# One Block instead of two, FFN weights turned by VectorE: an attention and FFN layer on one core

## The chip, the cores and the metric

The kernel runs on 1 core of one Trainium2 chip. The metric is the device time of one execution in microseconds. The engines of the core work side by side: PE (TensorE, matmul), ACT (ScalarE), DVE (VectorE), POOL (GpSimd) and SP (SyncE, which here only issues DMA transfers and waits for semaphores). Each engine runs its instructions strictly in order; a wait holds everything behind it on that engine.

## The reference, cut to what matters

```python
# x: (4, 512, 1024), ctx: (4, 64, 1024); 16 heads of 96 in 4 key/value groups
h = concat([ctx, layernorm(x)], axis=1)
q, k, v = layernorm(x) @ Wq.T, h @ Wk.T, h @ Wv.T
x = x + softmax(q @ k.T / sqrt(96)) @ v @ Wo.T
# FFN, INTER = 2752; w_gate, w_up: (2752, 1024), w_down: (1024, 2752)
def fake_quant(t, axis):
    s = maximum(max(abs(t), axis) / 127, 1e-8)
    return clip(round(t / s), -128, 127) * s
def qlinear(x, w):            # both sides scaled by row and rounded to integers
    return fake_quant(x, -1) @ fake_quant(w, 1).T
y = layernorm(x)
x = x + qlinear(silu(qlinear(y, w_gate)) * qlinear(y, w_up), w_down)
```

## The kernel before, in words

Everything is one launch with two phases, each a Block of its own with its own tensors in SBUF and PSUM; between the Blocks all engines meet.

**Attention** goes over 4 batches (one sequence of 512 tokens and 64 context rows each), and in a batch over 16 heads. Products of attention are done in three f16 matmuls (high and low halves: `three`, L819 to L821). A head has four tiles of 128 queries: scores (`score_tile`, L908 and L909) into one of two banks, VectorE's row maximum (L1117), ScalarE's exp (L1004), VectorE's reciprocal (L1122), GpSimd's scaling (L792), ScalarE's high half (L1015), GpSimd's low half (L797, L798), and a DMA transpose issued by SyncE (`turn_p`, L698), which the product with the values (`pv_tile`, L923 to L926) waits for. The projections of queries, keys, values and output of this and the next batch are spread between these (`side_work`).

**FFN weights are prepared beside attention.** There are 52 units: for each quarter of the intermediate columns 11 units of gate and up rows (`GU`; 10 of 128 rows and one of 96) with 1024 columns, and two of w_down rows with 2752 columns, which are worked in two halves of 1408 and 1344. A unit is loaded by SyncE (`stage`, L612), VectorE takes the row maxima (`tile_scale`, L1140) and from them the scale, ScalarE multiplies by its inverse and adds 1.5 x 2^23 (`lift`, L977), VectorE subtracts that constant and writes integers as bf16 (`round_off`, L1158), SyncE transposes them by DMA in blocks of 128 columns (`turn`, L653) and stores them in DRAM (`keep`, L664). There are 60 such pieces, 44 of 1024 columns and 16 halves. In the first batch four units are done, in the others 16 each, spread over the share of the batch that `WEIGHTS_FOR` names.

**What sets the order.** A planner at the head of the file gives each step a time on a modelled clock (`pe_times`, `stage_events`, `token_events`, `engine_events`) and sorts the steps by it, engine by engine (ACT_ORDER, DVE_ORDER, POOL_ORDER, SP_ORDER). The order of each engine's instructions is fixed by that; the times themselves are not kept.

**FFN** goes over 16 tiles of 128 tokens. The loops run so that the gates of tile t+2 come before the down product of tile t+1 on TensorE:

```python
gates(0, True)
gates(1)
down(0, True)
with pe.Fori(0, TILES - 2) as t:
    gates(t + 2)
    down(t + 1)
```

`gates` (L1388) has four quarters of three groups, each group 8 matmuls into one of four banks; the groups are 512, 512 and 384 columns wide (the last unit of a quarter has 96 rows, 32 columns of the third group are not read). `down` (L1401) has two halves of 22 matmuls. VectorE reads the groups with the scales (L1500, L1504, L1510, L1511), multiplies after ScalarE's Silu (L1429, L1520), takes maxima (L1525), rounds h (`h_part`, L1558, L1562), and does norm and rounding of a later tile between quarters (`x_stats`, `x_norm`, `x_quant`). SyncE loads tiles and transposes x and h by DMA (L1319, L1326). Ahead of the first gates stand, after the Block's start: 52 small transposes on TensorE and 17 copies on ScalarE that spread the weights' scales over all partitions (L1410, L1442), tile 0's norm, rounding and transpose, and the loads of the weights of quarters 1 to 3 (L1329) and of w_down (L1343). Quarter 0 is loaded in attention's last batch (`first_gates`).

Of the kernel before, what the change touches and what calls it, by code (L numbers as in the profile page):

```python
# [5 lines left out]
ALU = mybir.AluOpType  # L6
# [6 lines left out]
P = 128  # L13
B = 4
# [14 lines left out]
P_UP = 2.0 ** 9  # L29
SCALE = float(HD) ** -0.5  # L30
# [33 lines left out]
WEIGHTS_FOR = (1.0, 1.0, 1.0, 0.85)  # L64
# [3 lines left out]
PRO = VALUES + [("Q", 0, 0), ("Q", 0, 1)] + KEYS[:2] + [("Q", 0, 2)] + KEYS[2:4]  # L68
LATE_KEYS = [(*u, 0) for u in KEYS[4:]]
# [161 lines left out]

def stores_before(k, parity):
    return (k - parity + 1) // 2


LAND = 6.0
TOKEN_LEAD, TOKEN_STEP = 20.0, 10.0


def stage_events():  # L240

    act, dve, sp = [], [], []
    done, split, lifted, turned, kept = {0: 0.0, 1: 0.0, 2: 0.0, 3: 0.0}, 0.0, 0.0, [0.0], [0.0, 0.0]
    for n, (t, i) in enumerate(STAGE):
# [52 lines left out]
def engine_events():  # L297
# [3 lines left out]
    for b in range(B):  # L301
        for o in batch_order(b):
# [71 lines left out]

class Kept:


    def __init__(self, nc, ctx):
        def sb(name, shape, dt):
            return ctx.enter_context(nc.sbuf_tensor(name, shape, dt))  # L380

        self.ident = sb("ident", [P, P], F32)
        self.minus_half = sb("minus_half", [P, TT], F32)
        self.s_w = sb("s_w", [P, B * NUNIT], F32)
        self.w_first = sb("w_first", [P, 4 * QC * D], BF16)
        self.w_first_in = ctx.enter_context(nc.semaphore("w_first_in"))
        self.x2_out = ctx.enter_context(nc.semaphore("x2_out"))


def attention_phase(nc, x, ctxT, wqT, wkT, wvT, woT, w_gu, w_dn, x2, wq_c, wo_c, gu_q, dn_q, kept):  # L390
    with ExitStack() as ctx:
        def sb(name, shape, dt):
            return ctx.enter_context(nc.sbuf_tensor(name, shape, dt))

        def sem(name):
            return ctx.enter_context(nc.semaphore(name))

        def psum(name, shape, dt):
            return ctx.enter_context(nc.psum_tensor(name, shape, dt))

        ident, minus_half = kept.ident, kept.minus_half
        s_w, w_first, w_first_in, x2_out = kept.s_w, kept.w_first, kept.w_first_in, kept.x2_out
        x_acc = sb("x_acc", [P, TT, D], F32)
        xc = sb("xc", [P, 2, D], F32)
        xh = sb("xh", [P, 2, 2 * D], F16)
        stats = sb("stats", [P, 2, 6], F32)
        xnT = sb("xnT", [P, 2 * KD, S], F16)
        xnT_hi, xnT_lo = xnT[:, 0:KD, :], xnT[:, KD:2 * KD, :]
        w_in = sb("w_in", [P, 2, I], F32)
        wq2 = sb("wq2", [P, 2, 2, D], F16)  # L410
        wo2 = sb("wo2", [P, 2, 2, HALF], F16)

        wk_hi, wk_lo, wv_hi, wv_lo = [w_first[:, i * 3072:(i + 1) * 3072].bitcast(F16) for i in range(4)]
        q2 = sb("q2", [P, 2, 2, G, T], F16)
        k2 = sb("k2", [P, 2, KV, S], F16)
        v_hi = sb("v_hi", [P, ST, KV, HD], F16)
        v_lo = sb("v_lo", [P, ST, KV, HD], F16)
        p_f = sb("p_f", [P, NF, S], F32)
        p_nat = sb("p_nat", [P, NN, 2 * S], F16)
        pT = sb("pT", [P, 2, PB, T], F16)  # L420
        early = pT[:].rearrange("p j m t -> p (j m t)").bitcast(F32)
        early_wk, early_wq = early[:, 0:3072], early[:, 3072:3072 + D]
        ctx_in = xc[:, 0, 0:KD * C].rearrange("p (k c) -> p k c", k=KD)
        o2 = sb("o2", [P, 2, 2, QC, T], F16)
        o3 = sb("o3", [P, 2, T], F16)
        w_int = sb("w_int", [P, CUT], BF16)
        w_t = sb("w_t", [P, 2 * D], BF16)
        small = sb("small", [P, 48], F32)
        mean_var = small[:, 0:8].rearrange("p (t c) -> p t c", t=TT)
        var_eps, rstd = small[:, 8:12], small[:, 12:16]  # L430
        sums, inv_sum, neg_max = [small[:, a:a + 8].rearrange("p (j t) -> p j t", j=2) for a in (16, 24, 32)]
        w_amax, w_inv = small[:, 40:42], small[:, 42:43]

        ps_g = [psum(f"ps_g{i}", [P, 512], F32) for i in range(NG)]
        ps_s = [psum(f"ps_s{i}", [P, 1024], F32) for i in range(2)]
        ps_o = psum("ps_o", [P, 512], F32)

        consts = sem("consts")
        dconsts = sem("dconsts")
        x_in = [sem(f"x_in{t}") for t in range(TT)]  # L440
        acc_in = sem("acc_in")
        ctx_in_s = sem("ctx_in_s")
        w_in_s = [sem(f"w_in_s{i}") for i in range(2)]
        e_in = [sem(f"e_in{i}") for i in range(2)]
        e_up = sem("e_up")
        e_out = sem("e_out")
        h_up = sem("h_up")
        h_out = sem("h_out")
        w_up = sem("w_up")
        w_out = sem("w_out")  # L450
        w_small = sem("w_small")
        w_turned = sem("w_turned")
        w_stored = [sem(f"w_stored{i}") for i in range(2)]
        wq_kept = [sem(f"wq_kept{i}") for i in range(2)]
        wo_kept = [sem(f"wo_kept{i}") for i in range(2)]
        wq_in = [sem(f"wq_in{i}") for i in range(2)]
        wo_in = [sem(f"wo_in{i}") for i in range(2)]
        ln_st = sem("ln_st")
        ln_pow = sem("ln_pow")
        ln_y = sem("ln_y")  # L460
        x_hi_s = sem("x_hi_s")
        x_lo_s = sem("x_lo_s")
        xn_turned = [sem(f"xn_turned{t}") for t in range(TT)]
        g_done = sem("g_done")
        s_done = sem("s_done")
        mx_done = sem("mx_done")
        p_done = sem("p_done")
        p_high = sem("p_high")
        p_scaled = sem("p_scaled")
        p_low = sem("p_low")  # L470
        p_turned = [sem(f"p_turned{t}") for t in range(TT)]
        pv_done = sem("pv_done")
        ev_hi = sem("ev_hi")
        ev_lo = sem("ev_lo")
        q_moved = sem("q_moved")
        k_moved = sem("k_moved")
        ctx_hi = sem("ctx_hi")
        ctx_lo = sem("ctx_lo")
        v_up = sem("v_up")
        v_done = sem("v_done")  # L480
        inv_done = sem("inv_done")
        o_hi_s = sem("o_hi_s")
        o_lo_s = sem("o_lo_s")
        o_moved = sem("o_moved")
        acc_done = sem("acc_done")

        block = ctx.enter_context(nc.Block())

        def bank(use):
            return ps_g[AT[use] % NG]  # L490

        def filled(eng, use):

            eng.wait_ge(g_done, AT[use] + 1)

        def evacuated(eng, use):

            kind = use[1][0]
            if kind == "WO":
                eng.wait_ge(acc_done, ADDED[use] + 1)  # L500
            elif kind == "V":
                eng.wait_ge(v_done, VALUE[use] + 1)
            else:
                eng.wait_ge(ev_lo, SPLIT[use] + 1)

        def tile_no(b, t):

            return t if b is None else (b + 1) * TT + t

        def token_tile(b, t):  # L510

            return x_acc[:, t, :] if b is None else xc[:, t % 2, :]

        def halves(b, t):

            if b is None and t >= 2:
# [1139 lines left out]
```

## Time and profile before

| | us |
|---|---|
| median of 3 runs | 1663.08 |
| range of the runs | 1661.41 to 1667.41 |
| the profiled execution: its own time | 1660.82 |
| the profiled execution: its span | 1659.0 |
| attention's last output product added at | 1147.41 |
| a tile of the FFN's loop | 28.93 |

Busy times are those of each engine in the span or in a stretch; they overlap. A granted clock of 1.00 is TensorE's 2.4 GHz, and 0.5 is 1.2 GHz; a stretch's figure is a mean. The chain of waits is followed back from the last instruction, at each step to what released it; "SPq" in it is SyncE's queue, and "issue" is time in which the engine waited for nothing that the profile shows.

### The profile page before, as it was taken

To read this page: it belongs to the slowest core of one execution; us is meant where nothing else is said; L and a number is where in the kernel's file an instruction comes from. 1 tells how busy PE (TensorE), PEld (TensorE's weight loads), DVE (VectorE), ACT (ScalarE), POOL (GpSimd) and SP (SyncE) were. 2 spreads that over 40 slices of the span, in tenths; PEclk is the share of its full clock that TensorE was granted. 3 is DMA by queue.
4 is the path that set the end of the run, shared out by engine and by line. 5 is a ranking of instruction groups with operands and counts; after the bars stand their busy time and mean duration, and the time that the engine had idled before them with its cause. 6 is when DMAs were issued, how large, how long until landed. Compare 5 with 4: busy or idle time off the path is not lost.

```text
span 1659.0 us, 23906 instructions
## 1 busy us (share of the span) xinstructions
PE 1543.9 (93%) x8084; PEld 765.7 (46%) x8084; DVE 1031.0 (62%) x1952; ACT 644.0 (39%) x1180; POOL 637.7 (38%) x827
## 2 busy tenths in 40 slices
PE   6989989999988999999899899988599999999997
PEld 3544434654433465444355444444244444444443
DVE  5245564345574535566544557563589898998984
ACT  3366655146554315655523565562111111111110
POOL 3277786047766405767621576660000000000000
PEclk9999999999998999999999999999799999999999
DMA  7299999489999959999986999997923324233331
GB/s 247 69 247 230 232 251 238 145 222 229 247 234 224 243 170 220 234 224 257 235 208 188 285 241 255 207 232 213 364 62 81 104 65 102 80 82 103 81 92 56
DMA packets 529803, 310.92 MB, mean 187 GB/s; under 512 B 473904, under 2 KB 480816, under 8 KB 528560
## 3 DMA queue, kind: packets, MB, share of 16 engines
q1 hardware_dynamic: 529712, 309.76, 76.6%
q8 instruction: 50, 0.82, 0.2%
q14 instruction: 41, 0.34, 0.1%
HBM read 139.20 MB, written 46.66 MB: 112 GB/s over the span
## 4 chain that ended last, share of the span: by engine, by line
PE 62%; SPq 11%; DMA 9%; POOL 8%; ACT 4%; DVE 4%; issue 3%; ACTq 0%; DVEq 0%
PE ps_gu L1388 18%; PE ps_d L1401 10%; PE ps_g L819 8%; PE ps_g L821 8%; PE ps_g L820 8%; SPq L698 5%; PE ps_s L908 4%; POOL p_nat L797 3%; POOL p_f L792 3%; DMA pT<-p_nat 3%; PE ps_o L923 2%; PE ps_o L924 2%; PE ps_o L926 2%; SPq L680 2%; ACT p_nat L1015 1%
## 5 line engine op out<-in xcount | busy, mean ns | idle before, releaser
L797 POOL TENSOR_TENSOR p_nat<-p_f,p_nat 128x512 f16<-128x512 f32 x256 | 300.5, 1174 | 170.4 <-ACT p_nat L1015 169.4
L792 POOL TENSOR_SCALAR p_f<-p_f,small 128x576 f32<-128x576 f32 x256 | 205.3, 804 | 302.4 <-DVE small L1122 302.2
L1015 ACT ACTIVATE p_nat<-p_f 128x576 f16<-128x576 f32 x256 | 174.3, 681 | 243.6 <-POOL p_f L792 232.6
L908 PE MATMUL ps_s<-k,q 96*128 96x512 f16 x768 | 224.6, 385 | 40.5 <-ACT p_f L1004 40.4
L1117 DVE TENSOR_REDUCE small<-ps_s 128x1 f32<-128x576 f32 x256 | 191.8, 749 | 96.7 <-PE ps_s L909 95.8
L1004 ACT ACTIVATE p_f<-ps_s,small 128x576 f32<-128x576 f32 x256 | 186.8, 730 | 117.6 <-DVE small L1117 116.8
L1388 PE MATMUL ps_gu<-w_gu_sb,xT 128*128 128x512 bf16 (+1 forms) x1152 | 231.0, 361 | 1.0 <-DMA w_gu_sb<-gu_q 1.0
L1429 ACT ACTIVATE g_sb<-g_sb,sx 128x512 f32<-128x512 f32 (+1 forms) x128 | 74.5, 582 | 393.0 <-DVE g_sb L1500 336.1
L1367 POOL TENSOR_TENSOR rstd<-var_eps,minus_half 128x1 f32<-128x1 f32 x16 | 8.8, 548 | 458.5 <-DVE var_eps L1470 458.5
L1401 PE MATMUL ps_d<-w_dn_sb,hT 128*128 128x512 bf16 x704 | 162.5, 385 | 5.3 <-DMA hT<-h_int 5.3
L1388 PEld LDWEIGHTS ps_gu<-w_gu_sb,xT 128*128 128x128 bf16 x1152 | 112.7, 98 | 116.7 <-DMA w_gu_sb<-gu_q 1.4
L1122 DVE RECIPROCAL small<-small 128x1 f32<-128x1 f32 x256 | 40.6, 161 | 180.4 <-ACT p_f L1004 179.0
L819 PE MATMUL ps_g<-xnT,wq 128*128 128x512 f16 x384 | 147.6, 384 | 4.1 <-DVE wq L1070 2.2
L909 PE MATMUL ps_s<-k,q 96*128 96x64 f16 x768 | 148.5, 193 | 0.0
L819 PE MATMUL ps_g<-wo,o 128*128 128x512 f16 x384 | 147.8, 385 | 0.0
L923 PE MATMUL ps_o<-pT,v_lo 128*96 128x512 f16 x320 | 127.9, 400 | 21.1 <-DMA pT<-p_nat 19.5
L820 PE MATMUL ps_g<-wo,o 128*128 128x512 f16 x384 | 147.5, 384 | 0.0
L821 PE MATMUL ps_g<-wo,o 128*128 128x512 f16 x384 | 147.3, 384 | 0.0
L821 PE MATMUL ps_g<-xnT,wq 128*128 128x512 f16 x384 | 147.2, 383 | 0.0
L820 PE MATMUL ps_g<-xnT,wq 128*128 128x512 f16 x384 | 147.0, 383 | 0.0
L908 PEld LDWEIGHTS ps_s<-k,q 96*128 96x128 f16 x768 | 75.2, 98 | 140.4 <-issue 33.0
L1171 DVE SCALAR_TENSOR_TENSOR x_acc<-ps_g,x_acc 128x512 f32<-128x512 f32 x128 | 87.9, 687 | 62.6 <-PE ps_g L821 62.1
(113 smaller groups left out, 2467.7 us busy)
## 6 DMA issues: line engine op xcount, KB each, us to landing
w_in<-w_gu SPq DMA_DIRECT2D x40, 512.0 KB, 4.6
wq<-wq_c SPq DMA_DIRECT2D x36, 512.0 KB, 4.7
wo<-wo_c SPq DMA_DIRECT2D x24, 768.0 KB, 5.9
gu_q<-w_t SPq DMA_DIRECT2D x44, 256.0 KB, 4.2
w_in<-w_dn SPq DMA_DIRECT2D x8, 1376.0 KB, 7.1
w_gu_sb<-gu_q SPq DMA_DIRECT2D x3, 2816.0 KB, 12.6
x_acc<-x SPq DMA_DIRECT2D x4, 2048.0 KB, 8.5
x<-x_acc SPq DMA_DIRECT2D x8, 1024.0 KB, 5.1
```

The source lines that it names most:

```text
L792: nc.gpsimd.tensor_scalar(f, f, inv_sum[:, j % 2, t:t + 1], P_UP, ALU.mult, ALU.mult).then_inc(p_scaled, 1)
L797: nc.gpsimd.tensor_tensor(h[:, S + C:2 * S], f[:, 0:T], h[:, 0:T], ALU.subtract)
L819: nc.tensor.matmul(o, l_hi, r_hi, start=(first and i == 0), stop=False)
L820: nc.tensor.matmul(o, l_hi, r_lo, start=False, stop=False)
L821: mm = nc.tensor.matmul(o, l_lo, r_hi, start=False, stop=(last and i == len(pairs) - 1))
L908: nc.tensor.matmul(o[:, 0:T], l, k2[0:HD, hl, kv, 0:T], start=(i == 0), stop=(i == 2))
L923: nc.tensor.matmul(o, v_lo[:, t, kv, :], p[:, t, :], start=(t == 0), stop=False)
L1004: nc.scalar.activation(p_f[:, tile(b, j, t) % NF, :], scores(t), ACT.Exp, bias=neg_max[:, j % 2, t:t + 1], accum_out=sums[:, j % 2, t:t + ...
L1015: nc.scalar.activation(p_nat[:, t % NN, 0:S], p_f[:, tile(b, j, t) % NF, :], ACT.Copy).then_inc(p_high, 1)
L1117: nc.vector.tensor_reduce(neg_max[:, j % 2, t:t + 1], scores(t), AX.X, ALU.max, negate=True).then_inc(mx_done, 1)
L1388: mm = nc.tensor.matmul(ps_gu[n % NR][:, 0:nu * P], xT[:, k, :], w[:, u0:u0 + nu, k, :], start=(k == 0), stop=(k == KD - 1))
L1401: mm = nc.tensor.matmul(ps_d[h][:], hT[0:rows, c, :], w_dn[0:rows, 4 * h:4 * h + 4, c, :], start=(c == 0), stop=(c == IC - 1))
```

## The change

- Both phases stand in one Block. Their tensors share one area of SBUF (`Area`), in which those of the FFN are placed over those of attention that are done with first; the FFN's banks are `ps_s` and `ps_g`. Where a step writes over an attention tensor, it waits for the counters of attention.
- In the weight preparation, ScalarE rounds (`round_off`: it adds the negative constant) and reads with a stride of four floats, writing bf16 in runs of 32; VectorE then transposes 32 by 32 blocks (`turn`); SyncE only stores. The 60 DMA transposes and VectorE's 60 roundings go. Weights lie in DRAM and SBUF in groups of 32 columns: the gates' loads have runs of 512 bytes instead of 2048, and TensorE reads its moving operand in runs of 32 elements instead of 128.
- The third group of a quarter has 352 columns instead of 384.
- `WEIGHTS_FOR` of the last batch is 0.75 instead of 0.85.
- The scales go through one TensorE transpose, one ScalarE copy, one store and eight loads that broadcast.
- The loading of FFN tiles 0 to 2, norm, rounding and transposes of tiles 0 and 1 (`ln_tile`, `x_transpose`, `x_stats`, ...), the residual of tile 0, the scales and the loads of quarters 1, 2 and 3 (four pieces each) are steps of the planner, in the last batch of attention. The loads of w_down come after attention's last store.

```diff
-WEIGHTS_FOR = (1.0, 1.0, 1.0, 0.85)
+WEIGHTS_FOR = (1.0, 1.0, 1.0, 0.75)
...
             k = TURNS.index((g, h))
-            t = max(t, turned[-1] + LAND)
-            dve.append((t, "round", g, h))
-            wide = halves == 2 or (k and halves_of(TURNS[k - 1][0] % NUNIT) == 2)
-            t = max(t + 2.5, (kept[-1] if wide else kept[-2]) + LAND)
-            sp += [(t, "turn", k), (t + LAND, "keep", k)]
+            both = wide(k) or (k and wide(k - 1))
+            t = max(t, (kept[-1] if both else kept[-2]) + LAND - 1.0)
+            act.append((t, "round", g, h))
+            dve.append((t + 1.5, "turn", g, h))
+            sp.append((t + 3.0, "keep", k))
+            kept.append(t + 3.0)
...
+    sp += [(e - 64.0, "ln_tile", 0), (e - 43.0, "x_transpose", 0), (e - 42.0, "ln_tile", 1), (values + 4.0, "x_transpose", 1),
+           (values + 4.5, "ln_tile", 2), (values + 6.0, "res_tile", 0)]
+    dve += [(e - 54.0, "x_stats", 0), (e - 50.0, "x_norm", 0), (e - 47.0, "x_quant", 0), (e - 46.9, "next_x_scale"),
+            (e - 34.0, "x_stats", 1), (e - 30.0, "x_norm", 1), (e - 27.0, "x_quant", 1, EV)]
+    pool += [(e - 52.0, "x_power", 0), (e - 32.0, "x_power", 1)]
+    weights = max(values + 1.0, filled_at(last, ("WO", KV - 2, TT - 1, 1)) + 2.5)
+    begin = {1: filled_at(last, ("Q", KV - 1, QC - 1)) + 8.0, 2: max(t for t, what, *_ in sp if what == "keep") + 8.0}
+    sp += [(weights, "scales_in")]
+    for i in range(PIECES):
+        sp += [(begin[1] + 6.0 * i, "load_gates", 1, i), (begin[2] + 4.0 * i, "load_gates", 2, i),
+               (max(weights, begin[2] + 4.0 * PIECES) + 5.0 + i, "load_gates", 3, i)]
...
+        def round_off(g, h):
...
+            to = w_int[0:rows, 0:turned_to(k)[1]].rearrange("p (m k c) -> p m k c", m=4, c=32)
+            act.wait_ge(w_up, lifts(g, h))
+            act.wait_ge(w_turned, k)
+            ins = nc.scalar.activation(to[:, :, 0:blocks, :], w[:, 0:blocks * P].rearrange("p (k c m) -> p m k c", c=32, m=4),
+                                       ACT.Copy, bias=-MAGIC)
...
+        def turn(g, h):
...
+            dve.wait_ge(w_out, k + 1)
+            dve.wait_ge(w_stored[k % 2], stores_before(k, k % 2) * EV)
...
+            nc.vector.transpose(w_t[0:rows, at:at + width], w_int[0:rows, 0:width]).then_inc(w_turned, 1)
...
-                        nu = 4 if i < 2 else 3
-                        for k in range(KD):
-                            mm = nc.tensor.matmul(ps_gu[n % NR][:, 0:nu * P], xT[:, k, :], w[:, u0:u0 + nu, k, :],
+                    nb = 16 if i < 2 else 2 * TAIL // 32
+                    for k in range(KD):
+                        mm = nc.tensor.matmul(ps_gu[n % NR][:, 0:nb * 32], (xT0 if first else xT)[:, k, :],
+                                              w[:, n0:n0 + nb, k * 32:(k + 1) * 32],
```

## Rows read from the trace of the kernel before

**Rows 1.** The page: busy time by engine, and shares of the chain.
```profile
PE 1543.9 (93%) x8084; PEld 765.7 (46%) x8084; DVE 1031.0 (62%) x1952; ACT 644.0 (39%) x1180; POOL 637.7 (38%) x827
...
PE 62%; SPq 11%; DMA 9%; POOL 8%; ACT 4%; DVE 4%; issue 3%; ACTq 0%; DVEq 0%
```

**Rows 2.** By stretch: length, busy us (instructions), clock, DMA share, GB/s.
```profile
60.00:325.00 265.00, 246.86 (x1376) 127.71 (x1374) 135.89 (x246) 138.21 (x257) 161.79 (x201) 0.97 0.90 212
325.00:600.00 275.00, 259.20 (x1426) 132.90 (x1425) 147.59 (x283) 134.38 (x253) 154.89 (x201) 0.97 0.97 224
600.00:870.00 270.00, 255.26 (x1367) 126.60 (x1365) 147.17 (x285) 133.91 (x251) 155.54 (x201) 0.97 0.99 227
870.00:1147.40 277.40, 260.30 (x1391) 130.61 (x1388) 149.82 (x282) 134.97 (x249) 142.80 (x192) 0.96 0.96 229
...
1147.40:1166.30 18.90, 7.67 (x52) 5.32 (x53) 6.28 (x13) 8.93 (x20) 0.55 (x1) 0.82 0.85 264
1166.30:1200.70 34.40, 20.94 (x96) 9.60 (x96) 23.35 (x47) 4.66 (x8) 0.55 (x1) 0.85 1.04 386
```

**Rows 3.** The chain by line, in batch 2 (325 to 600), then batch 4.
```profile
by line: PE ps_g L819 14.7%; PE ps_g L821 14.6%; PE ps_g L820 14.6%; PE ps_s L908 10.1%; SPq L698 9.1%; PE ps_o L923 4.4%; PE ps_o L924 4.3%; PE ps_o L926 3.5%; SPq L680 3.4%; SPq L653 2.4%; DMA xc<-x 2.1%; issue 1.7%; POOL p_nat L797 1.7%;
...
by line: PE ps_g L819 11.6%; PE ps_g L821 11.6%; PE ps_g L820 11.6%; SPq L698 10.6%; DMA pT<-p_nat 6.1%; PE ps_s L908 5.8%; PE ps_o L923 3.5%; issue 3.5%; PE ps_o L924 3.3%; DMA w_in<-w_gu 3.2%; SPq L653 3.1%; POOL p_nat L797 2.9%; PE ps_o 
```

**Rows 4.** SyncE's issues of two lines: duration ns min/median/max.
```profile
L653 SPq DMA_TRANSPOSE w_t<-w_int x60: 1228/1304/3349, 105.3 to 1138.1; - x60
...
L698 SPq DMA_TRANSPOSE pT<-p_nat x256: 1241/1397/6693, 72.7 to 1121.4; - x128
```

**Rows 5.** Groups of instructions: busy us, mean ns, idle before.
```profile
L1158 DVE TENSOR_SCALAR w_int<-w_in 128x1024 bf16<-128x1024 f32 (+3 forms) x60 | 51.6, 860 | 25.7 <-DMA w_t<-w_int 24.5 <-ACT w_in L977 1.2
L779 POOL TENSOR_TENSOR xh<-xc,xh 128x1024 f16<-128x1024 f32 x12 | 25.5, 2125 | 0.0
L1479 DVE TENSOR_REDUCE x_max<-x_ln 128x1 f32<-128x1024 f32 x16 | 19.5, 1220 | 0.6
L1031 ACT ACTIVATE xh<-xc 128x1024 f16<-128x1024 f32 x12 | 12.5, 1045 | 0.0
L1493 DVE TENSOR_SCALAR x_int<-x_ln 128x1024 bf16<-128x1024 f32 x16 | 11.1, 694 | 1.9
```

**Rows 6.** Timeline at the seam: start us, us, instruction, idle before it.
```profile
1147.41 0.69 DVE L1171 SCALAR_TENSOR_TENSOR x_acc<-ps_g,x_acc 128x512 f32<-128x512 f32 x1 [1.25 <-PE ps_g L821]
...
1166.09 12.28 SPq L1343 DMA_DIRECT2D w_dn_sb<-dn_q  x4
...
1188.38 8.05 SPq L1319 DMA_TRANSPOSE xT<-x_int  x1
...
1200.74 4.43 PE L1388 MATMUL ps_gu<-w_first,xT 128*128 128x512 bf16 x13 [12.43 <-DMA xT<-x_int]
```

**Rows 7.** The chain in order of time, in a tile of the FFN's loop.
```profile
1231.19 19.12 PE ps_gu L1388 x96
1250.31 9.81 PE ps_d L1401 x44
```

**Rows 8.** VectorE's timeline in that tile.
```profile
1233.06 0.69 DVE L1500 TENSOR_TENSOR g_sb<-ps_gu,s_gu 128x512 f32<-128x512 f32 x1
1234.88 0.69 DVE L1504 TENSOR_TENSOR u_sb<-ps_gu,s_gu 128x512 f32<-128x512 f32 x1 [1.13 <-PE ps_gu L1388]
1236.08 0.34 DVE L1510 TENSOR_TENSOR u_sb<-ps_gu,s_gu 128x176 f32<-128x176 f32 x1 [0.51 <-PE ps_gu L1388]
...
1251.07 0.68 DVE L1500 TENSOR_TENSOR g_sb<-ps_gu,s_gu 128x512 f32<-128x512 f32 x1
...
1254.73 0.16 DVE L1548 TENSOR_REDUCE h_max<-h_max 128x1 f32<-128x4 f32 x1
...
1257.58 1.59 DVE L1562 TENSOR_SCALAR h_int<-h_sb 128x2752 bf16<-128x2752 f32 x1
```

**Rows 9.** The page's DMA issues: count, KB each, us to landing.
```profile
w_gu_sb<-gu_q SPq DMA_DIRECT2D x3, 2816.0 KB, 12.6
```

More of the change, by code:

```diff
@@ L372, in keys_use, with __init__, place, take @@
     return (None, KEYS[2 * c + 1]) if c < 2 else (0, LATE_KEYS[-1])
+class Area:
+    def __init__(self, nc, ctx, size):
+        self.nc = nc
+        ctx.enter_context(nc.sbuf_tensor("area", [P, size // 4], F32))
+        self.base, self.size = nc.sbuf_base - size, size
+        self.end, self.at = 0, {}
+    def place(self, name, shape, dt, start):
+        size = WIDTH[dt]
+        for n in shape[1:]:
+            size *= n
+        self.at[name], self.end = start, -(-(start + size) // 32) * 32
+        assert self.end <= self.size, name
+        return self.nc.alloc_sbuf_tensor_at(name, shape, dt, offset=self.base + start)
+    def take(self, name, shape, dt):
+        return self.place(name, shape, dt, self.end)
 class Kept:
@@ L384, in __init__ @@
         self.s_w = sb("s_w", [P, B * NUNIT], F32)
+        self.s_row = sb("s_row", [B * NUNIT, P], F32)
         self.w_first = sb("w_first", [P, 4 * QC * D], BF16)
[L386 to L516, printed above, removed]
-                return p_nat[:].rearrange("p n s -> p (n s)")[:, (t - 2) * 2 * D:(t - 1) * 2 * D]
-            return xh[:, t % 2, :]
-        def head(b, j):
-            return b * H + j
-        def tile(b, j, t):
-            return head(b, j) * TT + t
-        def group_of(j):
-            return j // G, HEADS[j % G]
-        def out_rows(j):
-            kv, g = group_of(j)
-            if g == G - 1:
-                return o3[0:HD, 0, :], o3[0:HD, 1, :]
-            return o2[0:HD, kv % 2, 0, g, :], o2[0:HD, kv % 2, 1, g, :]
-        def scores(t):
-            return ps_s[t % 2][:, 0:S]
-        def staged(eng, n):
-            eng.wait_ge(w_in_s[n % 2], (n // 2 + 1) * EV)
-        def freed(eng, n):
@@ new lines, in __init__, with attention_tensors @@
+        self.w_stored = [sem(f"w_stored{i}") for i in range(2)]
+        self.pv_done = sem("pv_done")
+        self.acc_done = sem("acc_done")
+        self.s_row_up = sem("s_row_up")
+def attention_tensors(area):
+    shapes = (
+        ("xc", [P, 2, D], F32),
+        ("xh", [P, 2, 2 * D], F16),
+        ("xnT", [P, 2 * KD, S], F16),
+        ("wq2", [P, 2, 2, D], F16),
+        ("w_in", [P, 2, I], F32),
+        ("w_int", [P, CUT], BF16),
+        ("w_t", [P, 2 * D], BF16),
+        ("v_hi", [P, ST, KV, HD], F16),
+        ("v_lo", [P, ST, KV, HD], F16),
+        ("q2", [P, 2, 2, G, T], F16),
+        ("k2", [P, 2, KV, S], F16),
+        ("p_f", [P, NF, S], F32),
+        ("p_nat", [P, NN, 2 * S], F16),
+        ("pT", [P, 2, PB, T], F16),
+        ("x_acc", [P, TT, D], F32),
+        ("wo2", [P, 2, 2, HALF], F16),
+        ("o2", [P, 2, 2, QC, T], F16),
+        ("o3", [P, 2, T], F16),
+        ("stats", [P, 2, 6], F32),
+        ("small", [P, 48], F32),
+    )
+    return [area.take(*shape) for shape in shapes]
@@ new lines, in store_x, with first_gates @@
+        def store_x(b, h):
+            sp.wait_ge(acc_done, ADDED[b, ("WO", KV - 1, TT - 1, h)] + 1)
+            c = slice(h * 512, (h + 1) * 512)
+            sp.dma_start(x2[b * T:(b + 1) * T, c].rearrange("(t p) d -> p t d", p=P), x_acc[:, :, c]).then_inc(
+                x2_out, EV)
+        def first_gates():
+            filled(sp, values_use(B - 1))
+            k = sum(1 for n, (_, what, *a) in enumerate(SP_ORDER) if what == "keep" and n < SP_ORDER.index(
+                next(e for e in SP_ORDER if e[1] == "first_gates")))
+            for i in range(2):
+                sp.wait_ge(w_stored[i], stores_before(k, i) * EV)
+            sp.dma_start(w_first[:, 0:GU * D].rearrange("p (n e) -> p n e", n=4 * GU),
+                         gu_q[0:GU].rearrange("u (i p) e -> p (u i) e", p=P)).then_inc(w_first_in, EV)
@@ L1206, in ffn_phase @@
-def ffn_phase(nc, x2, gu_q, dn_q, kept, out):
+                i = QUERY[use_of(n)]
+                if i >= 2:
+                    filled(act, QUERY_USES[i - 2])
+                act.wait_ge(wq_kept[i % 2], splits_before(i, i % 2) * EV)
+            elif kind == "o" and a[0]:
+                filled(act, out_done(a[0] * 2 + a[1] - 2))
+                act.wait_ge(wo_kept[a[1]], a[0] * EV)
+            nc.scalar.activation(split_to(n)[0], split_from(n), ACT.Copy, scale=W_UP).then_inc(h_up, 1)
@@ new lines, in context_hi @@
+        def context_hi(b):
+            act.wait_ge(ctx_in_s, EV if b is None else (b + 2) * EV)
+            if b is not None:
+                filled(act, values_use(b))
+            nc.scalar.activation(xnT_hi[:, :, T:S], ctx_in, ACT.Copy).then_inc(ctx_hi, 1)
+        run = {"split": w_split, "lift": lift, "round": round_off, "evac": evac, "exp": chances, "high": chances_hi, "out_hi": out_hi,
+               "tokens_hi": tokens_hi, "context_hi": context_hi}
+        act.wait_ge(dconsts, 3)
+        context_hi(None)
@@ L1208, in ffn_phase @@
+    return sync, gpsimd, tensor, scalar, vector
+def ffn_phase(nc, ctx, x2, s_d, gu_q, dn_q, kept, out):
     NR = 4
@@ new lines, in ffn_phase @@
+    h_sb = place("h_sb", [P, I], F32, kept.area.end)
+    h_int = place("h_int", [P, IC * P], BF16, kept.area.end)
+    hT = place("hT", [P, IC, P], BF16, kept.area.end)
+    w_dn = place("w_dn_sb", [P, 2, B * DN * 4, CUT // 4], BF16, kept.area.end)
+    assert at["w_dn_sb"] <= at["x_acc"] and kept.area.end <= at["stats"]
+    stats = sb("stats2", [P, 2, 6], F32)
+    mean_var = sb("mean_var2", [P, 2], F32)
+    var_eps = sb("var_eps2", [P, 1], F32)
+    rstd = sb("rstd2", [P, 1], F32)
+    x_max = sb("x_max", [P, 1], F32)
@@ new lines, in ffn_phase @@
+    dn_in = [sem(f"dn_in{q}") for q in range(B)]
+    s_out = sem("s_out")
+    s_gu_in = [sem(f"s_gu_in{q}") for q in range(B)]
+    s_dn_in = [sem(f"s_dn_in{q}") for q in range(B)]
+    ln_in = sem("ln_in")
+    res_in = sem("res_in")
+    out_s = sem("f_out")
+    x_small = sem("x_small")
+    x_pow = sem("x_pow")
+    x_q = sem("x_q")
+    x_turned = sem("x_turned")
+    h_turned = sem("h_turned")
+    h_pad = sem("h_pad")
+    gu_done = sem("gu_done")
+    gu_read = sem("gu_read")
+    silu_done = sem("silu_done")
@@ new lines, in sync, with store, h_transpose, load_down @@
+    def sync(sp):
+        steps = sync_steps(sp)
+        ln_tile, res_tile, x_transpose = steps["ln_tile"], steps["res_tile"], steps["x_transpose"]
+        def store(t):
+            sp.wait_ge(r_done, t * 2 + 4)
+            sp.dma_start(out[bass.ds(t * P, P), :], x_res[:]).then_inc(out_s, EV)
+        def h_transpose(t):
+            sp.wait_ge(h_q, t + 1)
+            sp.wait_ge(d_done, t * 2)
+            sp.nop(nofuse=True)
+            sp.dma_start_transpose(hT[:], h_int[:]).then_inc(h_turned, EV)
+        def load_down(q):
+            c, n = q % 2, B * DN // 2
+            first = q // 2 * n
+            sp.dma_start(w_dn[:, c, first * 4:(first + n) * 4, :],
+                         dn_q[c, first:first + n].rearrange("u (i p) e -> p (u i) e", p=P)).then_inc(dn_in[q], EV)
+        sp.wait_ge(kept.x2_out, EV * 2 * B)
+        for q in range(B):
+            load_down(q)
+        h_transpose(0)
+        with sp.Fori(0, TILES - 3) as t:
+            ln_tile(t + 3)
+            x_transpose(t + 2)
+            h_transpose(t + 1)
+            store(t)
+            res_tile(t + 1)
+        x_transpose(TILES - 1)
+        for t in (TILES - 2, TILES - 1):
+            h_transpose(t)
+            store(t - 1)
+            res_tile(t)
+        store(TILES - 1)
+        sp.wait_ge(out_s, EV * TILES)
```

1829 lines of the change are left out of this document (941 added, 888 removed).

## The prediction

> **What bounds the kernel now.** I read the page first, then busy time by stretch, the chain of waits, SyncE's issues, and last the seam between attention and the FFN instruction by instruction. The page says TensorE is busy for 93% of the span, but the chain that ended last is only 62% TensorE; the rest is SyncE's queue, DMA, GpSimd and issue time [rows 1]. So most of the time is TensorE's and a part can be had from whoever feeds it. The stretches show three regimes [rows 2].
>
> Attention, 60 to 1147.4 us, four batches: TensorE's idle time is 18.1, 15.8, 14.7 and 17.1 us, 66 us in all, and the granted clock of 0.96 to 0.97 costs some 3% of 1087 us, about 35 us more (the two overlap in part). The DMA share is 0.97, 0.99 and 0.96 in the batches in which FFN weights are prepared: the DMA engines are full. The chain of those batches has next to TensorE first of all SyncE issuing the transposes of the chances (9.1% of the second batch, 10.6% of the fourth) and SyncE issuing the transposes of the weights, L653 (2.4% and 3.1%) [rows 3]. An issue of L698 takes 1.24 us at least and 6.7 at most [rows 4]: SyncE is held while the DMA engines are behind.
>
> The seam: TensorE's last output product is added at 1147.41; gates(0) fills only 20.9 us of the 34.4 from 1166.3 on [rows 2], gates(1) starts at 1200.74, having waited 12.43 us for a transpose that SyncE took 8.05 us to issue behind the weights' loads [rows 6]. gates(1) ends at 1221.4 (the down product that follows it and 9.81 us later gates(2) at 1231.19 fix this) [rows 7].
>
> The FFN's loop: gates 19.12 us and down 9.81 us of TensorE with no gap, 28.93 us a tile [rows 7]; VectorE waits for TensorE only at the start of a tile, 1.13 and 0.51 us [rows 8]. TensorE bounds it, VectorE follows with 1.6 us to spare.
>
> **The change, part by part.** The sum is made against the profiled execution: span 1659.0, time 1660.8, so 1.8 us lie around the span; it stands 2.3 us below the median of the runs, 1663.1.
>
> (a) The third group of each quarter: 384 to 352 columns. 45,056 columns in 19.12 us are 0.424 ns a column [rows 7]. A tile loses 4 x 8 x 32 = 1024 columns, 0.43 us; VectorE's spare 1.6 us covers it. 16 tiles: 6.9 us.
>
> (b) The seam. The two Blocks become one; tile 0's norm, rounding and transpose, those of tile 1, the loads of quarters 1 and 2 and the scales are moved before attention's end, and the 52 transposes of scales and their 17 copies go, for one transpose, one copy, one store and eight broadcast loads. gates(0) can follow the last output product at once. But then gates(0) and gates(1) run back to back without a down product between them, and VectorE is late next. Replayed with the rows of a steady tile: VectorE's quarter takes 3.66 us (1251.07 to 1254.73), h's rounding 4.4 us (1254.73 to 1259.17), the next tile's norm some 5.4 us (21.67 us from 1233.06 to 1254.73, less 1.64 of waits and four quarters) [rows 8]. TensorE's quarter is 4.66 us. With T for attention's end: VectorE ends gates(0) at T+21.0, its rounding at T+25.7; TensorE has filled its four banks at T+25.0 and stops; from there VectorE's average quarter of gates(1), 3.66 + 5.4/4 = 5.0 us, sets the pace, and TensorE ends gates(1) at T+40.6, with a table load of 1.3 us in ScalarE's first Silu some 0.4 later: T+41. Before it was T+74.0. Gain 33.0 us; the 14 gates after it bring 14 x 0.43 = 6.0 of (a). If VectorE hid wholly, it would be T+37.3.
>
> What covers this: the loads. Scales (3.4 MB) are issued behind the last head's values, about 13 us before T by the planner's times, quarter 3 (2.8 MB) behind them. 2816 KB take 12.6 us [rows 9], 3.4 MB 9 us at the 386 GB/s of the stretch after the seam [rows 2]; with a tile load and half of x2 they end at about T+10 and are wanted at T+14. w_dn (5.6 MB, four loads) starts at T+5 and is wanted at T+41; the transpose of h is queued behind it on SyncE, whose four issues took 12.28 us before [rows 6]. Both fit. Uncovered, each microsecond late is one lost.
>
> (c) Weight preparation, 60 pieces, worth 66 pieces of 1024 columns (44 + 16 x 1.375). Gone: 60 DMA transposes, 1.30 us of SyncE each in the median, 1.23 at least [rows 4], more where the engines are full; some 85 us of SyncE and DMA in all, a tenth of batches 1 to 3. Gone from VectorE: the rounding, 51.6 us. New on VectorE: a 32 by 32 transpose of 128x1024 bf16. The trace has none. Nearest below, a rounding to bf16 of this size at 0.69 us; above, a reduction over 1024, 1.22 us [rows 5, 8]. I take 1.2: it moves every element once and I expect no faster rate. 66 x 1.2 = 79: +28 us on VectorE (-6 to +29), which is at 55% in these batches. New on ScalarE: rounding with a read stride of four floats. Nearest row: a 128x1024 copy to f16, 1.045 us; above, GpSimd's subtraction of that size, 2.125 us [rows 5]. I take 1.1, by the nearest row: +73 us (69 to 140), from 49% busy to 57% in batches 1 to 3.
>
> What the trace says of the stride is only that ScalarE's contiguous copy takes 1.045 us [rows 5]. The Trainium skill (Advanced Engine Details and Errata, SBUF Cachelines) speaks against the change here: a line is 16 bytes, two hits on it are needed for full rate, and these reads hit each line once. It names no factor; at twice the time ScalarE would have some 140 us more, and the sum would end at B's 1624 below; by the copy's row it stays 1610. No row shows a strided read. The skill (VectorE: DVE Perf Modes, The three transpose paths) has 311 ns for a 128x128 block transpose; eight of those would be 2.5 us, an estimate from that page, VectorE's +28 would be +113, and the sum again B's.
>
> Effect on attention: L653 on the chain is 6.6 us in the second batch and 8.6 in the fourth [rows 3], some 6 between: 21 us. In its place stand the handshake, ScalarE rounds, VectorE turns, SyncE stores, planned 1.5 us apart, where VectorE waits in order for ScalarE and holds row maxima and reciprocals, which hold exp and so the score banks. And SyncE's store waits for VectorE. I charge 7 us. Bounds: gain 45 (two thirds of idle and clock loss of batches 1 to 3, 48 and about 27 us) and loss 20. Taken: 14 us gained. It is nearer to L653's own share, because the transposes of the chances gain from emptier engines too.
>
> (d) The last batch's weights in 0.75 instead of 0.85 of it, and 5.6 MB of loads (25 us of DMA by [rows 9]) in its last 73 us. The pieces that ran to 1138 us before [rows 4] are gone there, so one replaces the other: 0, between -5 and +8. The stores' layout keeps 2 KB per partition; the loads go from 2 KB to 512 B runs, unpriced by any row, in (b)'s margin.
>
> (e) TensorE reads its moving operand in runs of 32 columns instead of 128: nothing. Pieces of 128 run at 0.424 ns a column at a granted clock of 1.00, that is 1.02 cycles of 2.4 GHz, so reading in pieces has cost at most 2%; the runs get four times as many. Taken 0, between 0 and E below.
>
> Sum: 33.0 + 6.0 + 14 = 53. Span 1606, time 1607.8; at the runs' median 1610.
>
> **The rivals.** B: attention gains nothing, since ScalarE and the handshake take back what DMA gives. Way: rounding on ScalarE at up to 2.1 us a piece, 140 us, 66% busy, with exp and the high halves behind it. For it: GpSimd has 8% and ScalarE 4% of the chain [rows 1]. Against: SyncE has 11%. Time 1660.8 - 39 + 2.3 = 1624; with 10 lost, 1634. C: attention is bound by the DMA engines throughout, and a tenth less load takes 40 us: 1584. For it: share 0.97 to 0.99. Against: idle and clock loss there are only 75 us. D: quarter 3's or the scales' small runs are late, or SyncE is caught by a wait of the moved steps (it waits in order for tile 0's rounding while chances wait behind it): 15 us, 1625. E, the slower side: reading in runs of 32 columns slows each matmul. Place: every gates and down, 140 a tile. It decides from 53/16 = 3.3 us a tile, 12% of 28.5. At 20%: 16 x 5.7 = 91 us, 1701. Against it: pieces of 128 cost nothing. That the third group stays as long would take 7 us back and is inside the forecast.
>
> **Numbers.** Forecast 0.46 (own range 1596 to 1619), B 0.25, C 0.15, D 0.09, E 0.05. Predicted 1610. The range 1584 to 1636 takes B, D and most of C. All but E are faster by over 0.5% (8 us, about what runs of this kernel can tell): faster 0.94, same 0.01, slower 0.05.
>
> **What would show it.** TensorE without a gap between the last output product and gates(0), the end of gates(1) at T+41 with a gap of 3 us inside it that VectorE's reads end; gates 18.7 us a tile (over 21 would be E). Attention's end near 1133; the DMA share of batches 1 to 3 at 0.9, L653 gone from the chain and L698's part smaller. The rounding on ScalarE at 1.1 us (2.1 would bear out the page), the block transpose at 1.2 us. Wrong if attention's end stays at 1147 or later (B), or SyncE stands in a wait within 60 us of its end (D).

## The result and the profile after

The changed kernel takes 1644.34 us (median of 4 runs, 1643.45 to 1647.58) against 1662.24 of the kernel before beside it: a ratio of 0.9895, 95% interval 0.9875 to 0.9914, some 18 us faster. Forecast were 1610 and a range of 1584 to 1636: the sign is right, the gain a third of what was forecast, the time outside the range. The profiled execution has a span of 1643.0 and a time of 1645.1.

The page after, busy time and chain, against [rows 1]; the chain names the banks `ps_s` and `ps_g` where the FFN's matmuls write now.

```profile
PE 1528.0 (93%) x8033; PEld 757.7 (46%) x8033; DVE 1056.7 (64%) x1952; ACT 756.7 (46%) x1230; POOL 620.6 (38%) x827
...
PE 56%; POOL 10%; ACT 10%; DVE 9%; issue 6%; DMA 4%; SPq 4%; ACTq 0%; DVEq 0%
```

SyncE's queue falls from 11% to 4% of the chain, as forecast; ScalarE rises from 4% to 10% and VectorE from 4% to 9%. ScalarE has 113 us more work, where my sum had 73 for the rounding alone.

By stretch, after, against [rows 2] (the same columns: length, busy PE, PEld, DVE, ACT, POOL, clock, DMA share, GB/s):

```profile
60.00:325.00 265.00, 245.32 (x1371) 126.96 (x1370) 137.59 (x245) 145.44 (x261) 160.40 (x201) 0.97 0.90 208
325.00:600.00 275.00, 257.67 (x1421) 131.04 (x1420) 154.16 (x283) 168.26 (x272) 149.84 (x201) 0.99 0.85 204
600.00:870.00 270.00, 248.35 (x1323) 121.59 (x1322) 152.02 (x279) 166.61 (x268) 149.33 (x201) 0.98 0.89 209
870.00:1140.00 270.00, 244.53 (x1322) 123.73 (x1320) 162.80 (x295) 180.39 (x278) 137.58 (x192) 0.95 0.88 218
```

The DMA share fell from 0.97 and 0.99 to 0.85 and 0.89 in the middle batches: the relief is there. But TensorE is busy for less of the same stretches (257.7 and 248.4 us, where it was 259.2 and 255.3), and ScalarE is at 61, 62 and 67% in the last three. Now the seam and the loop, from the chain in order of time:

```profile
1172.30 18.60 PE ps_s L1483 x96
...
1212.69 9.81 PE ps_g L1496 x44
1222.50 18.69 PE ps_s L1483 x96
1241.19 9.81 PE ps_g L1496 x44
```

Attention ends at 1172.3, 24.9 us later than before (1147.4); gates(0) begins at once, gates(1) ends 40.4 us after that, where it took 74.0; a tile takes 28.50 us instead of 28.93 [rows 7]. Each batch's last store shows where attention got longer: issued at 336.7, 616.6 and 896.9 us before, at 337.5, 617.8 and 903.4 after. The first two batches lose 1.2 us together, the third 5.3, the last 18.4.

The two new operations, by shape (columns as in [rows 5]):

```profile
L1028 ACT ACTIVATE w_int<-w_in 128x1024 bf16<-128x1024 f32 x40 | 82.0, 2051 | 0.1
L1218 DVE STREAM_TRANSPOSE w_t<-w_int 128x1024 bf16<-128x1024 bf16 x40 | 49.7, 1243 | 29.6 <-ACT w_int L1028 29.6
```

The block transpose takes 1.243 us (1.2 assumed). The rounding takes 2.051 us (1.1 assumed), the far end of the bounds of term (c).

### The profile page after: what moved, and what is told of

Its sections match the earlier page's. It is cut to its first block, busy times and chain, and to the rows that moved or that the text cites. A ratio compares the mean times of both kernels' runs of the same rounds, so it can differ in the third digit from the quotient of the medians.

```text
span 1643.0 us, 23811 instructions
## 1 busy us (share of the span) xinstructions
PE 1528.0 (93%) x8033; PEld 757.7 (46%) x8033; DVE 1056.7 (64%) x1952; ACT 756.7 (46%) x1230; POOL 620.6 (38%) x827
## 4 chain that ended last, share of the span: by engine, by line
PE 56%; POOL 10%; ACT 10%; DVE 9%; issue 6%; DMA 4%; SPq 4%; ACTq 0%; DVEq 0%
PE ps_s L1483 17%; PE ps_g L1496 10%; PE ps_g L854 7%; PE ps_g L856 7%; PE ps_g L855 7%; POOL p_nat L832 4%; POOL p_f L827 4%; PE ps_s L949 3%; ACT w_int L1028 3%; ACT p_f L1062 2%; ACT p_nat L1073 2%; SPq L736 2%; DVE small L1173 2%; DMA pT<-p_nat 2%; DVE w_t L1218 2%
## 5 line engine op out<-in xcount | busy, mean ns | idle before, releaser
L827 POOL TENSOR_SCALAR p_f<-p_f,small 128x576 f32<-128x576 f32 x256 | 199.2, 779 | 315.5 <-DVE small L1178 315.2
L1483 PE MATMUL ps_s<-w_gu_sb,xT 128*128 128x512 bf16 (+1 forms) x1152 | 226.2, 357 | 2.7 <-DVE g_sb L1582 2.7
L1496 PE MATMUL ps_g<-w_dn_sb,hT 128*128 128x512 bf16 x704 | 161.2, 382 | 5.3 <-DMA hT<-h_int 5.3
L1483 PEld LDWEIGHTS ps_s<-w_gu_sb,xT 128*128 128x128 bf16 x1152 | 112.4, 98 | 113.8 <-DVE g_sb L1582 7.0
L854 PE MATMUL ps_g<-xnT,wq 128*128 128x512 f16 x384 | 145.7, 379 | 3.3 <-DVE wq L1126 2.2
L856 PE MATMUL ps_g<-xnT,wq 128*128 128x512 f16 x384 | 145.5, 379 | 0.0
L855 PE MATMUL ps_g<-xnT,wq 128*128 128x512 f16 x384 | 145.4, 379 | 0.0
L1028 ACT ACTIVATE w_int<-w_in 128x1024 bf16<-128x1024 f32 (+3 forms) x60 | 132.3, 2205 | 0.1
```

Of the source, the lines that this page charges most:

```text
L827: nc.gpsimd.tensor_scalar(f, f, inv_sum[:, j % 2, t:t + 1], P_UP, ALU.mult, ALU.mult).then_inc(p_scaled, 1)
L854: nc.tensor.matmul(o, l_hi, r_hi, start=(first and i == 0), stop=False)
L855: nc.tensor.matmul(o, l_hi, r_lo, start=False, stop=False)
L856: mm = nc.tensor.matmul(o, l_lo, r_hi, start=False, stop=(last and i == len(pairs) - 1))
L1028: ins = nc.scalar.activation(to[:, :, 0:blocks, :], w[:, 0:blocks * P].rearrange("p (k c m) -> p m k c", c=32, m=4), ACT.Copy, bias=-MAGIC)
L1483: mm = nc.tensor.matmul(ps_gu[n % NR][:, 0:nb * 32], (xT0 if first else xT)[:, k, :], w[:, n0:n0 + nb, k * 32:(k + 1) * 32], start=(k == 0 ...
```

## The experiments

Every time stands beside runs of the kernel before on the same chip (1662.7 to 1664.3 us); ratios are against those. "Attention's end" is the end of its last output product in the profiled execution.

**e1: the weights' columns in DRAM in the rounding's order.** The host lays out the columns of each weight so that ScalarE reads in a row; the output is the changed kernel's.

```diff
+            to = w_int[0:rows, 0:turned_to(k)[1]].rearrange("p (m e) -> p m e", m=4)[:, :, 0:width // 4]
...
-            ins = nc.scalar.activation(to[:, :, 0:blocks, :], w[:, 0:blocks * P].rearrange("p (k c m) -> p m k c", c=32, m=4),
-                                       ACT.Copy, bias=-MAGIC)
...
+            nc.scalar.activation(to, w.rearrange("p (m e) -> p m e", m=4), ACT.Copy, bias=-MAGIC).then_inc(w_out, 1)
```

> The columns of w_gate, w_up and w_down lie in DRAM in the order in which the rounding writes them, so ScalarE's rounding reads without a stride and is one instruction; everything else is the changed kernel, and so is its output. Theory A (the strided read, 2.05 us for 1024 columns where a contiguous copy takes 1.05, is what attention lost): the rounding takes 1.05 to 1.15 us, ScalarE loses 62 us of work, attention's end moves from 1172 back to 1140 to 1150, and the time is 1612 to 1624. Rival B (the last batch lost because its weights are squeezed into 0.75 and the FFN's first steps and loads stand in it): attention's end 1164 or later, 1634 to 1642. Rival C (the handshake of three engines 1.5 us apart): ends near B's, with VectorE still waiting 40 us for the rounding.

Measured: 1616.53 us, ratio 0.9707 (0.9689 to 0.9724); attention's end 1141.9. The rounding:

```profile
L1027 ACT ACTIVATE w_int<-w_in 128x1024 bf16<-128x1024 f32 x40 | 41.9, 1047 | 0.1
```

Theory A holds in time and place: 30.4 us of attention come back for 67 us less on ScalarE (132.3 + 2.4 to 67.5), 16.1 of them before the last store of batch 3 and 14.3 after it. For 1024 columns the output lies in a row in both kernels, so the read stride is all that differs in the 44 gate and up pieces. What TensorE waits for the exp's banks, in the kernel before, after and e1 (total us, times, longest):

```profile
PE ps_s L908 <- ACT p_f L1004: 40.4, 23, 6.2
```

```profile
PE ps_s L949 <- ACT p_f L1062: 71.3, 45, 6.3
```

```profile
PE ps_s L949 <- ACT p_f L1056: 47.5, 30, 5.8
```

ScalarE works in order: each rounding of 2 us stands before an exp, and the exp holds one of two banks of scores. The same shows in SyncE's queue in the last batch, where the load of the next unit waits for the rounding to free its buffer; after, then e1:

```profile
SPq L665 <- ACT w_int L1028: 27.8, 8, 14.5
```

```profile
SPq L665 <- ACT w_int L1027: 9.7, 5, 3.8
```

**e5: the same work on ScalarE without the stride** (the edit against e1).

```diff
+            nc.scalar.activation(w, w, ACT.Copy).then_inc(w_again, 1)
+            act.wait_ge(w_again, k + 1)
             nc.scalar.activation(to, w.rearrange("p (m e) -> p m e", m=4), ACT.Copy, bias=-MAGIC).then_inc(w_out, 1)
```

> The contiguous rounding of e1_contig, with one more ScalarE instruction before each of the 60 roundings that copies the same columns in place (1.14 us for 1024): ScalarE has the work of the strided rounding again, and a little more, without a stride. Theory A as time on ScalarE: back to the changed kernel, attention's end 1168 to 1180 and 1640 to 1652. Rival A2 (the stride costs by what it does to other engines' access to SBUF, not by ScalarE's time): under 1628.

Measured: 1643.76 us, ratio 0.9890 (0.9873 to 0.9906), attention's end 1170.6: the changed kernel again. The copy takes 1.047 us. So the stride costs through ScalarE's time and through nothing else that could be seen; A2 (under 1628) falls.

**e12: a stride of two floats.**

```diff
+            nc.scalar.activation(w_int[0:rows, 0:width].rearrange("p (m c) -> p m c", m=2),
+                                 w.rearrange("p (c m) -> p m c", m=2), ACT.Copy, bias=-MAGIC).then_inc(w_out, 1)
```

> The changed kernel with ScalarE's rounding reading with a stride of two floats and writing 512 in a row instead of four floats and 32 in a row (the order of the weights' columns is not the reference's). By the rule that full rate needs two hits on a line of 16 bytes, a stride of 8 bytes is free: 1.05 us for 1024 and e1_contig's time, 1612 to 1621. If a stride as such costs: 2.05 us and 1640 to 1648.

Measured: 1617.87 us, ratio 0.9712 (0.9687 to 0.9737), attention's end 1144.6.

```profile
L1028 ACT ACTIVATE w_int<-w_in 128x1024 bf16<-128x1024 f32 x40 | 45.1, 1127 | 0.1
```

Stride of one float 1.047, of two 1.127, of four 2.051 us. A stride as such costs 8%; that of 16 bytes doubles the time.

**e2, e3, e8, e11: the last batch's share.** One number each, with the strided rounding (e2) or with e1's.

```diff
-WEIGHTS_FOR = (1.0, 1.0, 1.0, 0.75)
+WEIGHTS_FOR = (1.0, 1.0, 1.0, 0.85)
```

> The changed kernel with the last batch's weights spread over 0.85 of the batch again. Theory A (ScalarE's strided rounding): little, 1640 to 1646. Rival B (squeezing): attention's end moves some 8 to 12 us earlier, but the loads of quarters 2 and 3 come behind the last piece in the planner and so up to 10 us later against the gates; 1632 to 1640, with a gap in gates(0) that a load ends.

> Both edits: contiguous rounding and 0.85. Theory A: attention's end as with the contiguous rounding alone, within 3 us, and the time the same or up to 8 us more where quarters 2 and 3 land late in gates(0): 1614 to 1630. Rival B: the two gains add, under 1612 unless the loads come late.

> e1_contig with 0.80 of the last batch for the weights. At 0.75 attention ended at 1142 and the seam took 40.6 us; at 0.85 attention ended some 5 us earlier and the seam took some 14 more, for a load. At 0.80: attention's end 1138 to 1142, the load late by 3 to 8 us, 1616 to 1622.

> e1_contig with 0.70 of the last batch for the weights. Seam: no load late, 40.6 us. Attention: the last batch ended 5 us later at 0.75 than at 0.85; at 0.70 another 2 to 4 us. 1616 to 1621; under 1614 if loads still delay attention's end at 0.75.

| rounding | share | time | ratio (95%) | attention's end | gates(1) ends after it |
|---|---|---|---|---|---|
| strided | 0.75 (the changed kernel) | 1644.34 | 0.9895 (0.9875 to 0.9914) | 1172.3 | 40.4 |
| strided | 0.85 (e2) | 1655.40 | 0.9945 (0.9925 to 0.9966) | 1169.3 | 51.6 |
| in a row | 0.70 (e11) | 1622.13 | 0.9752 (0.9732 to 0.9772) | 1144.7 | 40.4 |
| in a row | 0.75 (e1) | 1616.53 | 0.9707 (0.9689 to 0.9724) | 1141.9 | 41.3 |
| in a row | 0.80 (e8) | 1623.15 | 0.9767 (0.9750 to 0.9783) | 1139.6 | 49.4 |
| in a row | 0.85 (e3) | 1625.54 | 0.9772 (0.9753 to 0.9791) | 1138.7 | 53.3 |

The squeezing in rival B falls in both rows. Attention ends 3 us earlier at 0.85, but those 3 us are not the squeezing's: e3 is 3.9 us ahead of e1 and e2 2.5 ahead of the changed kernel at the last store of batch 3, up to which ScalarE, VectorE, GpSimd and SyncE work in the same order in both. From there to attention's end it is 254.6 us at 0.75 and 255.3 at 0.85 in a row, 268.9 and 268.4 strided: no difference. It also says what a difference between two profiled executions is worth: 3 to 4 us of attention come and go with the same order of work. What 0.85 does cost is the seam: the loads of quarters 2 and 3, which stand behind the last piece, make it 11 to 12 us longer. I had misread that in e2's and e8's expectations (e2: 1655, expected at most 1646; e8: 1 us above its range); e11 too is 1 us above its range, e3 inside. In e3 TensorE waits for such loads:

```profile
PE ps_s L1477 <- DMA w_gu_sb<-gu_q: 9.7, 2, 6.0
```

0.75 is the best of these. e11 says least: its profiled execution took 1617.5 us, 4.7 less than its median, so 0.70 and 0.75 are told apart by the ratios alone.

**e4: more room in the planner between rounding, turning and storing.**

```diff
-            dve.append((t + 1.5, "turn", g, h))
-            sp.append((t + 3.0, "keep", k))
-            kept.append(t + 3.0)
+            dve.append((t + 3.5, "turn", g, h))
+            sp.append((t + 6.0, "keep", k))
+            kept.append(t + 6.0)
```

> The changed kernel with the planner's times of VectorE's turn 3.5 us and SyncE's store 6 us behind the rounding, instead of 1.5 and 3; strided rounding kept. Rival C (the handshake): VectorE's waits for the rounding fall from 49 us to under 15, attention's end 10 to 20 us earlier, 1625 to 1635. Theory A: VectorE was not late by these waits but ScalarE was; 1640 to 1646, with the waits gone and the time hardly moved.

Measured: 1649.20 us, ratio 0.9910 (0.9893 to 0.9926), outside both expectations. VectorE's waits for the rounding fell from 49 to under 7 us, as forecast, and attention's end came 6.6 us earlier (1165.7), less than the 10 to 20 of rival C: it was 11.9 us ahead at the last store of batch 3 and lost 5.3 of them in the last batch. The later stores also put the loads off (TensorE waits 7.1 us for one), and gates(1) ends 49.1 us after attention. So more room in the handshake brings attention some 7 us, and the run does not gain by it, because the same numbers of the planner start the loads.

**e6: the rounding back on VectorE, columns in e1's order.**

```diff
-            act.append((t, "round", g, h))
+            dve.append((t, "round", g, h))
...
+            nc.vector.tensor_scalar(to, w.rearrange("p (m e) -> p m e", m=4), MAGIC, None, ALU.subtract).then_inc(w_out, 1)
```

> Host order as in e1_contig, and the rounding on VectorE as in the kernel before, in front of its block transpose; ScalarE only scales. ScalarE loses 68 us, VectorE gets some 50, and the handshake ScalarE to VectorE is gone. If ScalarE in order is what attention still waits for: 1604 to 1613. If VectorE is as scarce: 1613 to 1622. Slower than 1622 if VectorE at over 60% busy holds maxima and reciprocals.

Measured: 1617.05 us, ratio 0.9718 (0.9695 to 0.9741), attention's end 1145.7: no difference from e1 that can be told, as expected if VectorE is as scarce. Here VectorE was at 62% in batches 2 and 3, ScalarE at 49 to 50%.

**e7, e9, e10: what each part costs by itself.** e7 is the kernel before without the 60 DMA transposes; e9 and e10 are e1 without the roundings or without the block transposes.

```diff
-                sp.dma_start_transpose(
+                sp.sem_inc(w_turned, EV)
```

> The kernel before with the 60 DMA transposes of the weights left out (the counter is raised without a transfer, what is stored is the empty tile, so the FFN's weights are not the reference's); the stores stay. It prices term (c)'s relief alone: by my sum 21 us gained plus some, 1635 to 1645. If the engines and SyncE had room for them: 1655 to 1663. If attention is DMA-bound throughout (rival C of the prediction): 1620 to 1630.

> e1_contig with the 60 roundings left out: ScalarE only raises the counter, VectorE turns the empty tile (the FFN's weights are not the reference's). ScalarE has 67 us less. If each microsecond of ScalarE costs attention at the rate of the strided rounding (65 us more cost 28): some 20 to 28 us gained, 1588 to 1597. If only the work above some level costs: under 10 us, 1607 to 1615.

> e1_contig with the 60 block transposes left out: VectorE waits as before for the rounding and the stores and raises the counter (the FFN's weights are not the reference's). VectorE has 81 us less, its waits stay. If VectorE's time costs as ScalarE's: 1588 to 1600. If VectorE, under 60% busy, has the room: 1608 to 1616.

| left out | time | ratio (95%) | attention's end | against |
|---|---|---|---|---|
| 60 DMA transposes (e7) | 1635.51 | 0.9831 (0.9814 to 0.9849) | 1123.3 | 1147.4 before: -24.1 |
| 60 roundings, 67.5 us (e9) | 1606.50 | 0.9657 (0.9636 to 0.9677) | 1133.8 | 1141.9 in e1: -8.1 |
| 60 block transposes, 80.8 us (e10) | 1605.86 | 0.9648 (0.9629 to 0.9667) | 1135.8 | 1141.9 in e1: -6.1 |

Batches 2 and 3 of e7, beside [rows 2]:

```profile
325.00:600.00 275.00, 261.30 (x1459) 134.25 (x1457) 153.46 (x289) 135.82 (x255) 155.19 (x201) 1.00 0.88 207
600.00:870.00 270.00, 256.57 (x1420) 131.09 (x1418) 146.34 (x283) 134.91 (x254) 155.67 (x201) 0.99 0.89 211
```

The DMA share falls by a tenth and attention gets 24 us shorter: the relief was sized rightly (21 us, in e7's expectation "plus some"). e7 takes the transposes from SyncE's queue and from the DMA engines at once; which of the two brings the 24 us it doesn't say. e9 and e10 lie between their two expectations, just below the range for an engine with room: the first 67 us of ScalarE's rounding cost attention 8 us (the median 10), the next 67 to 68 cost 29 to 30 (e1 against e5 and the changed kernel). The price of work on an engine that is at half load is not one price.

Where attention's time lies, by the last store of batch 3:

| | that store issued at | from there to attention's end |
|---|---|---|
| before | 896.9 | 250.5 |
| the changed kernel | 903.4 | 268.9 |
| e1 | 887.3 | 254.6 |
| e7 | 885.2 | 238.1 |
| e9 | 882.5 | 251.3 |
| e10 | 882.6 | 253.2 |

## Why the prediction was wrong

**(a), the third group.** Right: 18.69 us for gates instead of 19.12, 28.50 a tile.

**(b), the seam.** Right: T+41 was forecast, T+40.4 measured, 33.6 us gained instead of 33.0. TensorE's waits for VectorE's reads (2.7 us in three) are where the replay put them, the first at T+25:

```profile
PE ps_s L1483 <- DVE g_sb L1582: 2.7, 3, 1.2
```

The loads fitted with little to spare: in e1 TensorE waited 0.8 us for one of them; at 0.80 and 0.85 it waited 7.3 to 9.7 us, and the seam was 8 to 12 us longer.

**(c), weight preparation.** Here it failed: attention was to end near 1133 and ended at 1172.3, 39 us later, and the rest of the sum held. The relief is right (e7, 24.1 us). The failed step is "I take 1.1, by the nearest row": the strided rounding takes 2.05 us, so that ScalarE got 135 us and not 73. e1 prices that at 30.4 of the 39 us. I had both ends, 69 to 140 us, but carried only the low end into the sum. The charge, 7 us for ScalarE, VectorE and the handshake together, and the bound of 20 us lost had no case for 135 us, although the upper end of my own duration put ScalarE at 66%. Against e7's 1123.3, the changed kernel's attention ends 49 us later; that is what stood against the 7. (The gain in the bounds was misadded too: two thirds of 75 us are 50, not 45; no term hangs on it.)

With the rounding at 1.05 us it is 18.6, still 12 more than the charge: e1 is 1616.5, 6 over the forecast and inside the range. The last stores say where: e1 is 2.1 us behind e7 before the last batch and loses 16.5 in it. Leaving out the roundings or the block transposes shortens the last batch by 3.3 and 1.4 us only, and 0.85 by nothing. So some 12 us of it, give or take the 3 to 4 us between executions, are no work of weight preparation that a run priced. What else is new there are the moved FFN steps and the loads of quarters 1 and 2; with them the DMA share of the last batch is as high as it was with the DMA transposes (e1, then e7):

```profile
870.00:1140.00 270.00, 246.04 (x1306) 119.82 (x1304) 167.10 (x299) 154.54 (x268) 139.85 (x194) 0.98 0.98 245
```

```profile
870.00:1140.00 270.00, 250.95 (x1352) 126.14 (x1349) 152.78 (x290) 140.50 (x264) 144.34 (x193) 0.98 0.89 226
```

No run leaves them out, so that they are the cause is likely and not shown.

**(d)** I took 0, between -5 and +8. The squeezing costs attention nothing that can be told (e1 against e3, the changed kernel against e2) and spares the seam 11 to 12 us; the loads in runs of 512 bytes did no harm at the seam that could be seen. But if the 12 us above are the moved steps' and the loads', they belong here, "so one replaces the other: 0" is a second step that failed, and of the 18.6 us about 7 are left, which is the charge.

**(e)** Right: gates take 18.69 us for 44,032 columns, 0.424 ns a column as before; runs of 32 columns cost TensorE nothing.

**The rivals.** The result is B's mechanism, with the place as written (exp and the high halves behind the rounding), at a price of 25 us lost where B allowed 0 to 10. C did not happen (e7: 24 us, not 40), nor E. Of D the loads came in time, but its sign is there: within 60 us of attention's end SyncE stands in waits of the moved steps, 4.7 us ahead of a load of gates and, here, for the transpose of tile 1:

```profile
SPq L1380 <- PE ps_o L965: 5.3, 1, 5.3
```

What these waits cost is not separated; in the kernel before, SyncE waited 7.2 and 4.2 us there for other things.

The Trainium skill (Advanced Engine Details and Errata, SBUF Cachelines) had said it: full rate needs two hits on a line of 16 bytes. The measurements agree, 2.05 us at one hit a line and 1.13 at two, though two hits are still 8% slower than a read in a row. That section gives no factor; here it is 1.96. The row I set against it, a contiguous copy, says nothing about a stride, and so the rule deserved more than a chance inside B. The other estimate from the Trainium skill (VectorE: DVE Perf Modes, The three transpose paths), 2.5 us for a block transpose of 128x1024 from eight of 128x128, did not hold: 1.243. The fault was the multiplying: 1.243 us for 1024 columns and 1.642 for 1408 make 1.04 ns a column and 0.18 us for each instruction (an estimate from these two), and eight instructions would pay the 0.18 eight times.

**A version that beats both** is e1: 1616.5 us against 1644.3 and 1662 to 1664. What it changes is only how the host lays out columns that it lays out anyway; that reordering is outside the metric.

## What to carry to other kernels

When an operation moves to another engine, price its access pattern, not its size: where the only row is a contiguous one, carry the penalty that speaks against it into the sum as a case of its own. An engine at 50% busy that works in order between two others has little room for long instructions: the first 67 us cost an eighth of their length and the next 67 nearly half. Compare two profiled executions stage by stage: a difference that stands before the edited stage, where the order of work is the same, is not the edit's (here 3 to 4 us of attention). And where two things hang on one number of a planner (here the last piece's time also starts the loads), a change that helps one is judged by both.

## What the runs showed of the hardware

ScalarE, 128x1024, fp32 to bf16: 1.047 us read in a row, 1.127 with a stride of 8 bytes, 2.051 with 16 bytes, the output in a row in all three; the same at 96 partitions (2.048). VectorE's 32 by 32 block transpose of bf16 takes 1.243 us for 128x1024 and 1.64 for 128x1408. TensorE reads its moving operand in runs of 32 bf16 (64 bytes) as fast as in runs of 128, 0.424 ns a column in both. Sixty DMA transposes of 192 to 352 KB between SBUF tensors, SyncE's time for issuing them included, cost attention 24 us where the DMA share is 0.96 to 0.99, though TensorE waited for none of them directly.
